# The next head's weights scaled by PoolE instead of ScalarE, in a software-pipelined DeltaNet kernel

## The reference, cut to what matters

```python
qkv = jnp.einsum('btc,dc->btd', x, W_qkv)
z = jnp.einsum('btc,dc->btd', x, W_z)
...
qkv_c = sum((xp[:, j:j + Tq, :] * conv_w[:, j] for j in range(KC)))
...
def step(S, inp):
    q_t, k_t, v_t, b_t, d_t = inp
    Sk = jnp.einsum('bhi,bhipj->bhpj', k_t, S)
    dv = b_t[..., None] * (v_t - Sk)
    upd = jnp.einsum('bhi,bhpj->bhipj', k_t, dv)
    S = S * d_t[:, :, None, :, None] + upd
    o = jnp.einsum('bhi,bhipj->bhpj', q_t, S)
    return (S, o)
...
out = out * rms * norm_w
out = out.reshape(Bq, Tq, VD) * jax.nn.silu(z)
y = jnp.einsum('btd,cd->btc', out, W_out)
```

## Time and profile before

| | |
|---|---|
| median of 3 runs | 1903.93 us (1902.93 to 1905.59) |
| the profiled execution | 1904.61 us, its span 1902.9 us |
| granted clock of TensorE, mean | 0.990 |
| busy PE, PEld | 1819.9 us, 1499.0 us |
| busy DVE, ACT, POOL | 1760.3 us, 1662.2 us, 1579.1 us |

### The profile page before, as it was taken

The page is one execution under the profiler, slowest core; times in us unless marked ns, Lnnn a source line. Parts: engine busy times, 40 slices in busy tenths (PEclk is TensorE's granted clock), DMA queues, the critical chain, the costliest instruction groups (busy, mean ns, idle before and its releaser), DMA issues.

```text
span 1902.9 us, 64596 instructions
## 1 busy us (share of the span) xinstructions
PE 1819.9 (96%) x24518; PEld 1499.0 (79%) x24518; DVE 1760.3 (93%) x2905; ACT 1662.2 (87%) x3207; POOL 1579.1 (83%) x1403
## 2 busy tenths in 40 slices
PE   7799999999999999999999999999999999987999
PEld 6577788887788887788887778888778888876888
DVE  7899999999999999999999999999999999986987
ACT  7599999999999999999999999999999999985332
POOL 5588899888989988889988889998989998883452
PEclk9899999999999999999999999999999999998999
DMA  3111010101010110111010101001010100022000
GB/s 124 36 31 41 25 48 25 42 25 45 21 47 25 29 38 24 42 25 47 25 42 25 41 25 47 25 22 45 25 42 25 47 25 20 25 85 78 21 15 23
DMA packets 36595, 69.89 MB, mean 37 GB/s; under 512 B 7868, under 2 KB 16572, under 8 KB 33988
## 3 DMA queue, kind: packets, MB, share of 16 engines
q1 hardware_dynamic: 36292, 65.77, 11.1%
HBM read 62.86 MB, written 2.90 MB: 35 GB/s over the span
## 4 chain that ended last, share of the span: by engine, by line
POOL 54%; issue 19%; PE 15%; DVE 9%; ACT 2%; POOLq 1%; DMA 0%; DVEq 0%; SPq 0%; ACTq 0%
PE bank L729 13%; POOL e_b L563 7%; POOL kq L516 6%; POOL a_lo L578 6%; POOL pt L523 6%; POOL b_le L553 6%; POOL osc L591 5%; POOL w L508 4%; DVE ae L1936 3%; POOL a L610 3%; POOL ri L530 3%; DVE yl L1966 2%; POOL solv L625 2%; POOL solv L632 2%; PE bank L732 1%
## 5 line engine op out<-in xcount | busy, mean ns | idle before, releaser
L1911 DVE SCALAR_TENSOR_TENSOR cc<-bank,wc,cc 128x510 f32<-128x510 f32 (+2 forms) x768 | 535.9, 741 | 2.6
L729 PE MATMUL bank<-h,w 128*128 128x512 f16 (+1 forms) x1920 | 424.2, 362 | 7.3 <-POOL w L508 5.7
L729 PEld LDWEIGHTS bank<-h,w 128*128 128x128 f16 x1920 | 178.0, 99 | 144.2 <-DVE zg L2014 8.7
L516 POOL TENSOR_TENSOR kq<-cc,kq 128x1024 f16<-128x1024 f32 x64 | 137.0, 2141 | 127.1 <-ACT kq L1467 127.1
L1518 ACT ACTIVATE invT<-bank 128x512 f16<-128x512 f32 x384 | 234.8, 611 | 4.9 <-PE bank L729 4.9
L1966 DVE TENSOR_TENSOR yl<-bank,mask 128x512 f16<-128x512 f32 x320 | 218.9, 684 | 3.9 <-PE bank L729 3.9
L1513 ACT ACTIVATE inv<-bank 128x512 f16<-128x512 f32 x320 | 195.2, 610 | 11.2 <-PE bank L729 10.9
L1433 ACT ACTIVATE cc<-bank,wc 128x512 f32<-128x512 f32 x256 | 175.1, 685 | 20.8 <-PE bank L729 17.8
L729 PE MATMUL bank<-w,h 128*128 128x256 f16 x1536 | 190.9, 275 | 0.0
L729 PE MATMUL bank<-w,goT 128*128 128x256 f16 x1536 | 188.6, 273 | 0.0
L732 PE MATMUL bank<-ident,cc 128*128 128x128 f32 x1024 | 159.0, 278 | 24.0 <-ACT v L1495 22.4
(11 more groups left out here) (234 smaller groups left out, 5499.1 us busy)
## 6 DMA issues: line engine op xcount, KB each, us to landing
inv<-ident_store SPq DMA_DIRECT2D x64, 256.0 KB, 2.6
invT<-ident_store SPq DMA_DIRECT2D x64, 256.0 KB, 2.6
w_raw<-in_wh SPq DMA_DIRECT2D x15, 1032.0 KB, 5.0
out<-sol SPq DMA_DIRECT2D x16, 128.0 KB, 1.7
v<-in_x SPq DMA_DIRECT2D x3, 512.0 KB, 3.8
moving<-rank_store SPq DMA_DIRECT2D x64, 8.0 KB
standing<-rank_store SPq DMA_DIRECT2D x64, 8.0 KB
w_raw<-in_wgate SPq DMA_DIRECT2D x1, 1024.0 KB, 5.0
```

Source lines behind the costliest of these rows:

```text
L516: gp.tensor_tensor(kq16[:, 1].rearrange("p i t s -> p i (t s)"), cc[:, 0:2], kq16[:, 0].rearrange("p i t s -> p i (t s)"), ALU.subtract).t ...
L729: return mm(o_, l_, r_, start=start, stop=stop, skip_group_check=True)
L1911: V.scalar_tensor_tensor(dst, src, wc[:, par(s), i, 3 - j:4 - j], dst, ALU.mult, ALU.add).then_inc(sig(f"conv{i}"), 1)
```

## The change

ACT's in-place scaling and its wait are removed: ACT makes the 16-bit high part straight from the unscaled weights with the scale in the copy. POOL scales the quarter in place ahead of its subtraction and waits for its own result in between. Counts of `w_hi` and `w_lo` are adapted; the same is done to the four quarters of the first head in the setup. Besides, several operations change places in the written orders:

- POOL: `queries_rest(s1)` comes right behind `low_half(s1)`, ahead of the output's scaling.
- PE: `key_cross` ahead of `turn_values(0)`; `turn_keys` behind `level_rows(1)` and `level_right(0)`; `level_right(1)` ahead of `query_state`; `level_left(1)` behind `base_values(1)`; `level_left(4)` ahead of `level_right(4)`.
- ACT: `values_turned(0)` behind `cross_kept` and `inverse_left(0)`; `inverse_right(0)` ahead of `squares(0)`; `squares(1)` ahead of `inverse_right(1)`; `decay_exp(1)` behind `inverse_right(2)`; `inverse_right(3)` ahead of `split_weights`; `high_half` ahead of `inverse_right(4)`.
- DVE: `squared_norms(0)` behind `second_rest`; `add_output(0)` behind `output_sums`; `add_output(1)` behind `level_rows(4)`. The group `z_gate(0)`, `decayed_queries`, `z_gate(1)`, `first_inverse` goes from the start of a body to the end of the one before, which is the same place in DVE's order except in the first and the last bodies (in the first body `decayed_queries` now comes ahead of `decayed_keys`).

```diff
@@ load_weights, on SP @@
-                need(sp, "w_lo", count * 4)
+                need(sp, "w_lo", count * 8)
@@ split_weights, on POOL (the setup's first_weights_low is changed in the same way) @@
-                need(pool, "w_hi", (head(s) + 1) * 8 + 2 * q + 2)
+                need(pool, "w_hi", (head(s) + 1) * 4 + q + 1)
                 qs_ = slice(q * 512, q * 512 + 512)
+                gp.tensor_scalar(w_raw[:, qs_], w_raw[:, qs_], W_SCALE, None, ALU.mult).then_inc(sig("w_lo"), 1)
+                pool.wait_ge(sig("w_lo"), (head(s) + 1) * 8 + q * 2 + 1)
                 gp.tensor_tensor(w16[:, to, 1, qs_], w_raw[:, qs_], w16[:, to, 0, qs_], ALU.subtract).then_inc(sig("w_lo"), 1)
@@ body, on POOL @@
                     low_half(s1)
+                    queries_rest(s1)
...
                 if s1:
-                    queries_rest(s1)
                     values_half(s1)
@@ project, on PE @@
-                    need(pe, "w_lo", (head(s) + 1) * 4 if head(s) else 2)
+                    need(pe, "w_lo", (head(s) + 1) * 8 if head(s) else 4)
@@ body, on PE @@
+                    key_cross(s1)
                     need(pe, 'iv', N(s1) + 1)
                     turn_values(0, s1)
-                    key_cross(s1)
                     level_left(0, s1)
...
+                if s1:
+                    level_right(1, s1)
                 if s2:
                     query_state(s2)
-                if s1:
-                    level_right(1, s1)
-                    level_left(1, s1)
                 if s0:
                     need(pe, 'vv', N(s0) * 2)
                     turn_queries(s0)
                 if s2:
                     base_values(1, s2)
+                if s1:
+                    level_left(1, s1)
...
+                    level_left(4, s1)
                     level_right(4, s1)
-                    level_left(4, s1)
@@ weights_high, on ACT @@
-                A(w_raw[:, qs_], w_raw[:, qs_], ACT.Copy, scale=W_SCALE).then_inc(sig("w_hi"), 1)
-                act.wait_ge(sig("w_hi"), head_ * 8 + 2 * q + 1)
-                A(w16[:, to, 0, qs_], w_raw[:, qs_], ACT.Copy).then_inc(sig("w_hi"), 1)
+                A(w16[:, to, 0, qs_], w_raw[:, qs_], ACT.Copy, scale=W_SCALE).then_inc(sig("w_hi"), 1)
@@ body, on ACT @@
                 if s0:
                     decay_exp(0, s0)
+                if s1:
+                    inverse_right(2, s1)
+                if s0:
                     decay_exp(1, s0)
-                if s1:
-                    inverse_right(2, s1)
...
                     inverse_left(4, s1)
+                if s0:
+                    high_half(s0)
+                if s1:
                     inverse_right(4, s1)
-                if s0:
-                    high_half(s0)
@@ body, on DVE @@
-                if s3:
-                    add_output(0, s3)
                 if s2:
                     output_sums(s2)
...
                 if s3:
-                    add_output(1, s3)
+                    add_output(0, s3)
                 if s1:
                     level_rows(4, s1)
```

More of the change, by code:

```diff
@@ L380, in _ @@
             load_turned_inverse(STEPS - 1)
-            sp.wait_ge(sig("w_lo"), NK * 4)
+            sp.wait_ge(sig("w_lo"), NK * 8)
             sp.wait_ge(sig("wc"), NK)
@@ L468, in first_weights_low @@
             def first_weights_low(q):
-                pool.wait_ge(sig("w_hi"), 2 * q + 2)
+                pool.wait_ge(sig("w_hi"), q + 1)
                 qs_ = slice(q * 512, q * 512 + 512)
+                gp.tensor_scalar(w_raw[:, qs_], w_raw[:, qs_], W_SCALE, None, ALU.mult).then_inc(sig("w_lo"), 1)
+                pool.wait_ge(sig("w_lo"), q * 2 + 1)
                 gp.tensor_tensor(w16[:, 0, 1, qs_], w_raw[:, qs_], w16[:, 0, 0, qs_], ALU.subtract).then_inc(sig("w_lo"), 1)
@@ L841, in z_rows @@
                 if N(s) == 0:
-                    pe.wait_ge(sig("w_lo"), 4)
+                    pe.wait_ge(sig("w_lo"), 8)
                 for t in range(2 * h, 2 * h + 2):
@@ L1141, in body @@
                     first_values(s2)
+                if s1:
+                    level_rows(1, s1)
+                    level_right(0, s1)
                 if s0:
@@ L1144, in body @@
                     turn_keys(s0)
-                if s1:
-                    level_rows(1, s1)
-                    level_right(0, s1)
                 if s2:
@@ L1670, in body @@
                 if s1:
-                    values_turned(0, s1)
                     cross_kept(s1)
                     inverse_left(0, s1)
+                    values_turned(0, s1)
                 if s2:
                     first_kept(s2)
+                if s1:
+                    inverse_right(0, s1)
                 if s0:
                     squares(0, s0)
-                if s1:
-                    inverse_right(0, s1)
                 if s2:
@@ L1694, in body @@
                     inverse_left(1, s1)
-                    inverse_right(1, s1)
                 if s0:
                     squares(1, s0)
+                if s1:
+                    inverse_right(1, s1)
                 if s3:
@@ L1706, in body @@
                     decay_exp(0, s0)
-                    decay_exp(1, s0)
                 if s1:
                     inverse_right(2, s1)
+                if s0:
+                    decay_exp(1, s0)
                 if s2:
@@ L1713, in body @@
                     inverse_left(3, s1)
+                    inverse_right(3, s1)
                 if s0:
@@ L1716, in body @@
                 if s1:
-                    inverse_right(3, s1)
                     z_tanh(0, s1)
                     inverse_left(4, s1)
-                    inverse_right(4, s1)
                 if s0:
@@ L1723, in body @@
                 if s1:
+                    inverse_right(4, s1)
                     z_tanh(1, s1)
@@ L2035, in gate_weights_low @@
             def gate_weights_low(q):
-                dve.wait_ge(sig("w_hi"), NK * 8 + q + 1)
+                dve.wait_ge(sig("w_hi"), NK * 4 + q + 1)
                 qs_ = slice(q * 512, q * 512 + 512)
@@ L2041, in up_weights_low @@
             def up_weights_low(q):
-                dve.wait_ge(sig("w_hi"), NK * 8 + 4 + q + 1)
+                dve.wait_ge(sig("w_hi"), NK * 4 + 4 + q + 1)
                 need(dve, "left_ps", STEPS * YL)
@@ L2155, in first_body @@
                 dve.wait_ge(sig("mask_steps"), 5)
+                decayed_queries(s0)
                 decayed_keys(s0)
                 dve.wait_ge(sig("gate_dma"), 32)
+                first_inverse(s0)
             def body(s0, s1, s2, s3):
@@ L2162, in body @@
                     return first_body(s0)
[L2163 to L2170, removed]
                 if s0:
@@ L2194, in body @@
                     level_rows(1, s1)
-                if s0:
-                    squared_norms(0, s0)
                 if s2:
@@ L2202, in body @@
                 if s0:
+                    squared_norms(0, s0)
                     convolve(2, 1, s0)
@@ L2243, in body @@
                         guard_gates()
+                if s3:
+                    add_output(1, s3)
+                if s0:
                     decayed_keys(s0)
+                if s1:
+                    z_gate(0, s1)
+                if s0:
+                    decayed_queries(s0)
+                if s1:
+                    z_gate(1, s1)
+                if s0:
+                    first_inverse(s0)
                 if s1 and (not s0):
@@ L2253, in last_bodies @@
             def last_bodies(s0, s1, s2, s3):
[L2254 to L2257, removed]
                 if s2:
```

## The result

The changed kernel takes 1999.47 us (median of 4 runs, 1997.21 to 1999.74) where the kernel before, in the same session, took 1903.43: a ratio of 1.050 (95% interval 1.0482 to 1.0518), 96 us slower. Forecast were 1945 us and a range up to 1972. The direction was right, the size was not.

A forecast was written before the change was run, and what follows sets the result against it. A 25.74 us PE-ACT-POOL loop bounded the kernel; the POOL loop, 23.55, would reach 26.50 through scaling (+0.75) and moved `queries_rest` (+2.08). At +2.75 a head over 15 heads: 1945 us, range 1909 to 1972.

The forecast's parts named there:

- The bound is a loop through several engines, not an amount of work: Ordinary body of 25.74 us: no engine is always busy, and the last head, with less ACT and POOL work, gains nothing.
- POOL loop B: PE's `base_values(1)`, ACT's `decay_exp(1)`, POOL from `decay_beta` through `unit_system` and output scaling to `rest_half`: 23.55 before, 26.50 forecast.
- 2.08 for the moved operation: `queries_rest`, moved on POOL between `low_half` and `output_scale`, adds 2.08 us start to start to the POOL loop.
- the new wait of "1.2 to 1.7" before `decay_beta`: POOL would wait 1.2 to 1.7 us there for ACT's `decay_exp`, while its 1.6 wait before `pairs_low` goes.
- the head's last body costs no more than the others: The 0.28 us extra of a head's last body would disappear under the POOL loop, making it 26.5 too.
- Scaling on POOL: 512-element scaling ahead of the subtraction: 0.65 us plus 0.10 wait, +0.75 in the loop; bounds 0.23 and 1.17.
- What it leaves behind gives nothing: At `queries_rest`'s old place POOL would reach `decay_beta` early and stand idle about 1.5 us for ACT.
- loop C: Not in the forecast: POOL `pairs_low` through `key_norm` to `unit_system`, PE's levels, ACT to `pairs_high`, and back; 25.74 before.
- A: Forecast's loop of now: PE `base_values(1)` to `z_rows(0)`, ACT `z_tanh(0)` to `pairs_high`, POOL `pairs_low` and `rest_half`; 25.74.
- `high_half` waits 0.2: ACT, with `high_half` ahead of `inverse_right(4)`, would wait about 0.2 us for DVE's matrix, making its loop about 25.95.
- PE would wait 0.7 before `turn_system`: Among PE's longest waits for POOL in the changed profile: 0.7 us here, 0.5 to 0.8 before `base_values(1)`.
- ACT gains nothing: ACT loses 0.64 us of scaling per body, but this is fully covered, as the last head showed.

The follow-up runs named there:

- The product: Changed kernel with POOL's scaling as a TENSOR_TENSOR product with a constant column instead of a TENSOR_SCALAR: 1968.46 us, ratio 1.0333.

## Why the prediction was wrong, step by step

- *The bound is a loop through several engines, not an amount of work*: right. The changed body is idle in part on every engine, and the last head's bodies, without the scaling, are 25.86 (POOL's next `pairs_low` rows there):

```profile
1749.61 2.13 POOL L520 TENSOR_TENSOR kq<-cc,kq 128x1024 f16<-128x1024 f32 x1 [0.25 <-ACT kq L1470]
1775.46 2.13 POOL L520 TENSOR_TENSOR kq<-cc,kq 128x1024 f16<-128x1024 f32 x1 [0.25 <-ACT kq L1470]
```

- *The POOL loop B becomes the bound*: right, term by term. 6.13 was forecast to the end of `decay_exp(1)` and 6.12 measured; 2.08 for the moved operation and the new wait of "1.2 to 1.7" before `decay_beta` (1.69) as well; and the head's last body costs no more than the others.
- *"Scaling on POOL ... I take 0.65 ... In the loop +0.75"*: **this step failed.** The scaling takes 1.51, and with its waits on both sides the way from the start of `gate_output` to the start of the subtraction is 972.61 - 968.55 = 4.06, where it was 2.32 before: 1.74, which is 0.99 more than the 0.75 of the forecast. The remaining terms came out slightly shorter, so that the body is 27.43 where 26.50 was forecast, 0.93 more; 58 bodies have this length, 54 us, and added to 1945 that is the 1999 measured. The upper bound was wrong in kind: I took the subtraction of the same size for a ceiling (1.17, and 1.28 from start to start) and the cast for the likely value, because scaling reads one operand. The product, which reads two, is cheaper than the scaling with one. Counting operands doesn't price an operation of POOL. The trace of before had a sign of it: of two TENSOR_TENSORs of 8 elements in `output_scale`, the sum takes 0.20 and the power 1.67 (L587 and L591).

  The Trainium skill (GPSIMD Engine Reference) gives 769 ns for 512 elements in the best case (Performance versus the Vector engine) and calls one-operand work roughly line-rate (Engine selection). This trace does not agree for a TENSOR_SCALAR: it takes 1.51 us, twice the first figure, and the measurement decides.
- *"What it leaves behind gives nothing"* (of `queries_rest`): incomplete, without effect on the sum. POOL does stand idle for ACT there, 1.69 us. But the move relieves loop C, which I hadn't seen, of 2.08; without that C would have set the body at 27.50, as it does in the kernel with this operation put back (2017.61 us). I had found the last head's body unchanged and concluded that POOL's stretch ahead of `unit_system` had slack. It shows only that this stretch may get shorter for nothing: A, of the same length, holds the body then. Made longer it counts at once.
- *`high_half` waits 0.2*: wrong place. No such wait is listed. Loop A did get 0.12 longer. The waits of a body name one of PE's weight loads for `add_output(0)`, which the change puts later; the first two lines are the waits for POOL in front of `turn_system` and `base_values(1)`:

```profile
PEld bank L733 <- POOL a L614: 1.6, 1, 1.6
...
PE bank L733 <- POOL solv L636: 0.7, 1, 0.7
...
PEld bank L733 <- DVE y_acc L2037: 0.2, 1, 0.2
```

  It stands in front of `z_rows(0)`, in loop A. PE's rows of a body of the last head:

```profile
1760.96 0.40 PE L733 MATMUL bank<-inv,a 128*128 128x64 f16 x8
1761.40 1.48 PE L733 MATMUL bank<-w,h 128*128 128x256 f16 x12
```

  Before, the same matmuls stood 0.23 ahead of `z_rows(0)` at 918.07:

```profile
917.84 0.40 PE L729 MATMUL bank<-inv,a 128*128 128x64 f16 x8
```

  Now `z_rows(0)` starts 0.44 behind them. The 0.21 more, with 0.06 less on ACT, is about the growth of the loop.

- *PE would wait 0.7 before `turn_system`*: it waits 1.6 there (weight loads), 0.9 more, which is about what the scaling was priced too low.
- *ACT gains nothing*: nothing speaks against it. Its busy time fell from 24.40 to 24.00 while the body grew, and no loop found here goes through its scaling; no run took the scaling off ACT alone.

What stays open: the 11 us of the exchanged orders alone (1913.56) are explained only to a half by the bodies, which take 25.85 and at a head's end 26.05, a head 103.6 against 103.25: 15 x 0.35 = 5 us. The profiled execution, 1909.85 us, is 5 above the one of before; the other runs of that kernel reach 1916.54, and no profile shows those.

## What to carry to other kernels

In a software pipeline over engines that are all nearly full, write down every loop by way of the waits, with its length, before moving work: an engine's wait is slack only for those loops that contain it, and a part whose removal changes nothing may still cost in full when it grows, because two loops of equal length hold the body. Work goes where all loops through it have room; here the same 1.5 us operation cost some 86 us in one place (1999.47 against 1913.56, with the same orders and the scaling on ACT) and some 17 in another (1931.06 against 1913.56). And an operation that no row shows on that engine deserves a bound much wider than its neighbours', or a row of its own first.

## What the runs showed of the hardware that was not expected

POOL's TENSOR_SCALAR with a constant costs 0.2 us and 2.5 ns an element (0.87 us for 256, 1.51 for 512), its TENSOR_TENSOR with a constant column 1.05 us for 512, its cast 0.61.

The clock of TensorE. In the kernel with the queries' low part put back, ten of the fifteen bodies that end a head take 27.8 and five 29.2. Windows of one of the long ones, whole and in part, and PE's timeline at two such places:

```profile
1021.97:1051.19 29.22, 26.45 (x365) 21.52 (x363) 24.96 (x41) 24.46 (x50) 24.79 (x21) 0.94 0.17 57
```

```profile
1039.00:1042.40 3.40, 3.15 (x23) 1.80 (x24) 0.27 (x2) 0.69 (x1) 3.32 (x4) 0.59 0.68 232
```

```profile
928.93 1.46 PE L733 MATMUL bank<-h,w 128*128 128x512 f16 x6 [1.95 <-POOL w L512]
```

```profile
1039.25 2.39 PE L733 MATMUL bank<-h,w 128*128 128x512 f16 x6 [1.96 <-POOL w L512]
```

In both bodies PE had waited about 1.95 us for the low weights. In one the six matmuls behind it take 1.46 us at the full clock (1.00 from 928 to 932), in the other 2.39, with a mean granted clock of 0.59 from 1039.00 to 1042.40, so most of it at the lower of the two levels, 1.2 GHz. The second body is 1.4 us longer than the first for this alone. Over all heads, in the profiled executions:

| kernel | PE's wait for the low weights | heads in which the matmuls behind it are slowed |
|---|---|---|
| changed | 1.40 to 1.43 | 0 of 15 |
| low part of the queries put back | 1.92 to 2.00 | 5 of 15 |
| only the scaling moved | 2.15 to 2.24 | 8 of 15 |

PE's waits of 1.6 for `unit_system` in the ordinary bodies of the last two kernels left the clock at full. So the longer of these waits also cost clock, 1.4 us each time it happened here. What decides between two waits of the same length was not tried.
